# One stream of bodies through six layers: the feed-forward in pieces between the attention's tiles

## The reference, cut to what matters

```python
def layer(x):
    x = x + attn_layer(shift_tokens(x))
    return x + ffn_layer(shift_tokens(x))
# shift_tokens: channels 64 to 127 come from the token before
# attn_layer: q, k, v = x @ Wqkv; q and k to unit length, scaled, rotated;
#   each window of 32 tokens looks at itself and the window before it:
#   softmax(q @ k.T * 8 + mask) @ v; then @ Wo
# ffn_layer: xn = layernorm(x) * g + b; a, gate = split(xn @ W1 + b1)
#   (a * gelu(gate)) @ W2 + b2
```

## Time and profile before

| | us |
|---|---|
| median of three runs | 7222.45 |
| the profiled execution, its own time | 7208.77 |
| its span, first to last instruction | 7206.7 |
| mean granted TensorE clock over the span | 0.823 of 2.4 GHz |

### The profile page before, as it was taken

The page is one execution under the profiler, slowest core; times in us unless marked ns, Lnnn a source line. Parts: engine busy times, 40 slices in busy tenths (PEclk is TensorE's granted clock), DMA queues, the critical chain, the costliest instruction groups (busy, mean ns, idle before and its releaser), DMA issues. The chain is left out here.

```text
span 7206.7 us, 178920 instructions
## 1 busy us (share of the span) xinstructions
PE 5312.7 (74%) x69288; PEld 3368.6 (47%) x69288; DVE 3840.9 (53%) x6202; ACT 3985.0 (55%) x8451; POOL 2396.7 (33%) x1351
## 2 busy tenths in 40 slices
PE   1000198888888888977777988888888979687778
PEld 0000065655656564733333655656564747343444
DVE  5555654645455554555554645455554546445854
ACT  4333264646455555539997646555554546355655
POOL 0000162626354444504443626354453535000000
PEclk6555599999999999976666989999998989766876
DMA  1000121212222121200000212212121212000000
GB/s 43 0 0 0 37 51 48 55 49 54 53 49 59 42 53 50 57 11 1 1 1 20 55 47 53 54 45 52 47 57 44 57 45 57 18 2 3 0 2 6
DMA packets 177838, 248.52 MB, mean 34 GB/s; under 512 B 51692, under 2 KB 79848, under 8 KB 175080
## 3 DMA queue, kind: packets, MB, share of 16 engines
q1 hardware_dynamic: 177128, 237.68, 13.2%
HBM read 43.50 MB, written 5.24 MB: 7 GB/s over the span
## 5 line engine op out<-in xcount | busy, mean ns | idle before, releaser
L377 PE MATMUL PS<-arena 128*128 128x512 f32 x2304 | 1163.5, 632 | 220.0 <-ACT arena L500 117.1
L670 POOL TENSOR_TENSOR arena<-arena 128x512 f32<-128x512 f32 x384 | 586.6, 1551 | 651.3 <-DVE arena L622 651.3
L670 POOL TENSOR_TENSOR lns<-arena 128x512 f32<-128x512 f32 x384 | 566.1, 1498 | 666.7 <-DVE arena L622 666.7
L377 PEld LDWEIGHTS PS<-arena 128*128 128x128 f32 x2304 | 412.9, 199 | 646.1 <-issue 359.7
L499 ACT ACTIVATE arena<-PS 128x512 f32<-128x512 f32 x768 | 472.1, 615 | 333.4 <-PE PS L377 258.4
L434 PE MATMUL PS<-arena 64*64 64x32 f32 x24576 | 534.7, 227 | 155.4 <-ACT arena L531 121.4
L592 DVE TENSOR_REDUCE arena<-PS 128x16 f32<-128x1024 f32 x192 | 235.2, 1225 | 731.0 <-PE PS L408 731.0
L1106 PE MATMUL PS<-arena 128*128 128x512 f32 x8 | 6.7, 1019 | 807.8 <-DVE arena L1040 807.8
L434 PEld LDWEIGHTS PS<-arena 64*64 64x64 f32 x24576 | 509.5, 141 | 191.7 <-issue 188.0
L611 DVE TENSOR_REDUCE arena<-arena 128x32 f32<-128x2048 f32 x192 | 438.8, 2285 | 293.4 <-ACT arena L500 286.1
L539 ACT ACTIVATE arena<-PS 128x512 f32<-128x512 f32 x384 | 208.9, 597 | 648.0 <-PE PS L434 648.0
(11 more groups left out here) (254 smaller groups left out, 11101.2 us busy)
## 6 DMA issues: line engine op xcount, KB each, us to landing
arena<-arena SPq DMA_DIRECT2D x2880, 64.0 KB, 2.0
arena<-in_L_ffn_Wqkv SPq DMA_DIRECT2D x12, 1536.0 KB, 6.5
arena<-in_L_ffn_Wo SPq DMA_DIRECT2D x48, 128.0 KB, 6.3
scratch<-arena SPq DMA_DIRECT2D x4, 1024.0 KB, 4.8
arena<-scratch SPq DMA_DIRECT2D x4, 1024.0 KB, 7.6
arena<-in_L_ffn_W SPq DMA_DIRECT2D x12, 341.0 KB
arena<-in_ffn_scales SPq DMA_DIRECT2D x12, 128.0 KB, 5.8
arena<-in_L_ffn_W SPq DMA_DIRECT2D x12, 128.0 KB
```

The lines of the kernel that those rows point to most:

```text
L377: pe.matmul(PS[:, QKV + n % 2, :], xs[uu % 2][:, par * P:(par + 1) * P], w, start=True, stop=True).then_inc(qkv_ready, 1)
L670: last = pool.tensor_tensor(heads(t2)[:, :, a:a + 32], heads(raws[par])[:, :, b:b + 32], sine, ALU.mult)
```

## The change

All six layers of a call run as one stream, with no meeting between them. `body` is called for b = 0 to 3 of each layer, one after the other, with the work ahead reaching into the next layer. The feed-forward of the 512 tokens of body g - 1 (one chunk) runs in pieces inside body g. After the last body of the call the last chunk's feed-forward runs by itself.

- **TensorE.** The order in a tile is written out by hand for each of the four tiles. Projection chunks and turns alternate. `mean` and `variance` stand in tile 0, three `gate` pieces in tile 1, three `value` pieces in tile 2, two `down` pieces (256 tokens each) in tile 3; all use the two banks of the projection. Chunks 4 and 5 of a projection move behind the head products. The first half of `project` moves ahead of the second scores. The mask matmuls go.
- **ScalarE** writes the masks into the score banks (`write_mask`), makes the shifted copies, squares, takes the logarithm and exponential for one chunk in place in PSUM, copies the gates out with their bias, and takes gelu in two instructions from SBUF to SBUF, with a table load before and one behind. It copies v and takes the inverse norms at the end of a tile instead of before the probabilities. The three thirds of the next layer's `Wqkv` are loaded from its queue.
- **VectorE** centres, normalises (two instructions), gates and adds for one chunk a body. `unit_length` moves behind `softmax_shift` and `add_stream`.
- **GpSimd** does the sine product in one instruction over both halves, with the input's halves swapped. It makes the next layer's tables in the stream.
- **SP** puts the loads of scales, `Wo`, `W1` and `W2` between the windows' copies of the next bodies, each behind a wait for the last reader of the old weights.
- Outside the block some semaphores of `attn_a` are merged into others.

The diff, cut to its core. TensorE, tile 0 and the parts of the others that differ:

```diff
-            def body(g, final):
-                for tt in range(TILES):
...
+            def body(run, b, feed, final):
+                g = run * BODIES + b
+
+                chunk_read(g, 2, 4)
+                qkv(run, b, 3, 0, 0)
+                turn_qk(g, 1, 0)
+                chunk_read(g, 2, 5)
+                qkv(run, b, 3, 1, 1)
+                turn_qk(g, 1, 1)
+                chunk_read(g, 3, 0)
+                qkv(run, b, 3, 2, 0)
+                turn_qk(g, 1, 2)
+                if feed:
+                    chunk_read(g, 3, 1)
+                    mean(g, 1)
+                turn_qk(g, 1, 3)
+                chunk_read(g, 3, 2)
+                qkv(run, b, 3, 3, 0)
+                turn_probs(g, 0, final)
+                scores(g, 1, 0)
+                if feed:
+                    mean_read(g)
+                    variance(g, 1)
+                heads(g, 0, 0, final)
+                heads(g, 0, 1, final)
+                chunk_read(g, 3, 3)
+                qkv(run, b, 3, 4, 0)
+                scores(g, 1, 1)
...
+                qkv(run, b, 3, 5, 1)
...
+                turn_probs(g, 1, final)
+                scores(g, 2, 0)
...
+                    gate(run, b, 1, 1)
+                if feed:
+                    gate_read(g, 0)
+                    gate(run, b, 2, 0)
+                heads(g, 1, 0, final)
+                heads(g, 1, 1, final)
+                project(run, b, 0, 0)
...
+                    qkv(run, b, 4, 4, 1)
+                scores(g, 2, 1)
+                project(run, b, 0, 1)
...
+                heads(g, 2, 0, final)
+                heads(g, 2, 1, final)
+                if feed:
+                    value_read(g, 0)
+                    value(g, 2, 1)
...
+                    down(run, b, 1, 1)
+                heads(g, 3, 0, final)
+                heads(g, 3, 1, final)
+                project(run, b, 1, 0)
...
-            with pe.Fori(0, BODIES - 1) as it:
-                body(run * BODIES + it, False)
-            body(run * BODIES + BODIES - 1, True)
...
+            body(first, 0, False, False)
+            with pe.Fori(0, DEPTH - 1) as l:
+                for b in range(1, BODIES):
+                    body(first + l, b, True, False)
+                body(first + l + 1, 0, True, False)
```

The new functions of ScalarE, and its order in a tile:

```diff
+            def write_mask(g, tt):
+
+                S = PS[:, SCORE:SCORE + 2, :].rearrange("p s (m e) -> p (s m) e", e=FD)
+                act.activation(S, masks[:, tt % 2:tt % 2 + 1, :].broadcast_to([P, FH, 2 * WIN]), ACT.Copy)\
+                   .then_inc(mask_ready, 1)
...
+            def gelu(g):
+                act.wait_ge(gate_copied, nth(g - 1, M, M - 1))
+                act.activation(gl[:, 0:M - 1, :], gl[:, 0:M - 1, :], ACT.Gelu)
+                act.activation(gl[0:DIM[M - 1], M - 1, :], gl[0:DIM[M - 1], M - 1, :], ACT.Gelu).then_inc(gelu_ready, 1)
+                log_exp_tables(act)
...
                     if further:
-                        copy_qkv(g, tt + 3, (0, 1), True)
+                        copy_qkv(g, tt + 3, 0, PROJECTION_BANK[tt][0], True)
+                    if ahead:
+                        copy_turned(g, tt + 1, 0)
                     exps(g, tt)
+                    if further:
+                        copy_qkv(g, tt + 3, 1, PROJECTION_BANK[tt][1], True)
+                    if reload and tt == 0:
+                        load_projection(l, 0)
+                    if feed and tt == 0:
+                        shift(g, b)
                     if ahead:
-                        copy_turned(g, tt + 1, (0, 1))
+                        copy_turned(g, tt + 1, 1)
                     if further:
-                        copy_qkv(g, tt + 3, (2, 3), True)
+                        copy_qkv(g, tt + 3, 2, PROJECTION_BANK[tt][2], True)
                     if ahead:
-                        copy_turned(g, tt + 1, (2, 3))
+                        copy_turned(g, tt + 1, 2)
+                        write_mask(g, tt + 1)
+                        copy_turned(g, tt + 1, 3)
...
+                    if feed and tt == 0:
+                        square_centred(g)
+                    if feed and tt == 1:
+                        copy_gate(g, 0, 0)
                     copy_probs(g, tt, final)
+                    if feed and tt == 2:
+                        gelu(g)
```

VectorE, GpSimd and SP:

```diff
                 for tt in range(TILES):
+                    ahead = not (final and tt + 1 >= TILES)
+                    further = not (final and tt + 3 >= TILES)
                     softmax_norm(g, tt, nth(g, TURN_PER, place_probs(tt - 1, 1, False)))
-                    if not (final and tt + 3 >= TILES):
+                    if feed and tt == 0:
+                        centre(g, 1)
+                    if further:
                         norms(g, tt + 3)
-                        unit_length(g, tt + 3)
-                    if not (final and tt + 1 >= TILES):
...
+                    if ahead:
                         softmax_shift(g, tt + 1)
                     if tt % 2 == 1:
-                        add_stream(g, it, tt // 2)
...
+                        add_stream(g, b, tt // 2)
+                    if further:
+                        unit_length(g, tt + 3)
...
-                    for half in range(2):
-                        a, b = half * 32, 32 - half * 32
-                        sine = table[:, 2 + k, par:par + 1, a:a + 32].broadcast_to([P, FH, 32])
-                        last = pool.tensor_tensor(heads(t2)[:, :, a:a + 32], heads(raws[par])[:, :, b:b + 32], sine,
-                                                  ALU.mult)
-                    last.then_inc(t2_ready, 1)
+                    halves = lambda a: a.rearrange("p h (s e) -> p h s e", s=2)
+                    sine = halves(table[:, 2 + k, par:par + 1, :]).broadcast_to([P, FH, 2, 32])
+                    pool.tensor_tensor(halves(heads(t2)), halves(heads(raws[par]))[:, :, ::-1, :], sine, ALU.mult)\
+                        .then_inc(t2_ready, 1)
...
+                for tt in range(TILES):
+                    windows(g + 4, tt, False)
+                    if tt == 1:
+
+                        wait_alone(sp, o_ready, nth(g + 3, HEAD_PER, 9))
+                        load_output(ds(l + 1, 1))
```

More of the change, by code:

```diff
@@ L644, in fa_vector @@
[L644 to L656 removed]
+                norms(first * BODIES, tt)
@@ L872, in program @@
+            for b in range(2, BODIES):
+                for tt in range(TILES):
+                    windows((first + DEPTH - 1) * BODIES + b, tt, False)
         HD8 = 8
```

784 lines of the change are left out of this document (502 added, 282 removed).

## The result

The changed kernel takes 6547.9 us (median of 4 runs, 6545.28 to 6550.86) beside 7223.65 for the kernel before on the same chip: ratio 0.9065, 95% interval 0.9054 to 0.9076. The forecast was 6600. The profiled execution has a span of 6543.5 us, 663.2 less than before.

What follows compares the result with a forecast made beforehand. TensorE was taken to set the pace. Fills, 79.0 us bodies and ends made 1947.8 us a call, 654 us less over both; 7 back for the second call and 20 for borders gave 6600 us, range 6440 to 6850 (0.75).

Steps and rivals of the forecast that it cites:

- 8.7 against 7.7 us, just covered: First half of a tile: TensorE issues 8.7 us, ScalarE needs 7.7, so ScalarE is just covered except in tile 0.
- The body: One new steady body on TensorE, counted against an old one of 71.1 us: 79.05, taken as 79.0 us.
- Feed-forward pieces: One chunk's up-projection, down-projection, mean and variance on TensorE lengthen each body by 9.45 us.
- -2.4 of filled waits: Four TensorE waits of 0.6 us before the head products, now filled by feed-forward pieces: minus 2.4 us a body.
- Masks: Eight mask matmuls of 0.31 us leave TensorE, ScalarE writes the masks instead: minus 2.5 us a body.
- Output projection: Tiles 1 and 3: its first half waits for ScalarE's copy of the heads, 0.6 plus 0.2 us: plus 1.6 a body.
- Tile 0: ScalarE's two shift copies (0.96 us) stand ahead of the mean and stall TensorE: plus 0.6 us a body.
- VectorE and GpSimd: Normalised probabilities meet GpSimd's first sine product, delaying their turn about 0.3 us a tile: plus 1.2 a body.
- Gelu path and table loads: ScalarE's gelu and table switches in second halves: tightest in tile 2, 0.4 us a body, counted as nothing; 0.5 kept for range.
- Borders: Ten layer borders inside calls: new tables and weight loads cost 2 us each (bounds 0 and 8), 20 us in all.
- Ends of a call: Fill 45.65 us, first body without feed-forward 70.2, last body running dry 73.9, last chunk's feed-forward alone 20.
- TensorE never waits: Rival, chance 0.07: a body is TensorE's busy time alone, 74.6 us, giving 6390 us.

Runs made afterwards that it cites:

- up_twice: The changed kernel with each of the six up-projection pieces of a chunk issuing its matmul twice: 6754.78 us, ratio 0.9356.

## Why the prediction was right, and where its terms were off

By its steps:

- **What bounds it** held: TensorE sets the body, busy 76 of 78.1 to 79.6 us, and added work on it shows at eight to nine tenths (up_twice). It left out that ScalarE sets it as well: its 0.78 us more a tile showed at nine tenths too. My "8.7 against 7.7 us, just covered" compared the sums of a whole half. It took no account of the order within it: the second turned probabilities wait for a bank that ScalarE empties only behind the mask write, so of the 1.0 us 0.3 were left in tiles 1 and 2 and nothing in tile 0.
- **The body**, 79.0: measured 78.14 in the second call, 79.4 in most of the first. Feed-forward pieces: +9.45 of work, 8.3 in busy time; right as "what TensorE issues". The time it costs against no pieces at all is 3.5, since the -2.4 of filled waits was one of several such waits. I had added that waits return without pieces only for the head products, not for the turns. And it is luck that 79.0 came out so near. By my terms (71.1 - 2.5 + 1.6 + 1.2) a body of the stream without pieces has 71.4 us, and the pieces add 7.6 (9.45 - 2.4 + 0.6). Measured are 75.4 in the mean and 3.5: the first is 4 us too low, the second 4 too high, and they cancel. Of the first 4 us I estimate, from the waits and runs above, about 1 for the head products' gaps without a holder, 1.3 to 2.1 for the masks' term, and 0.5 for the jumps, which I had put at the borders; the rest is open.
- **Masks**, -2.5: mis-sized. Starts give 0.22 us each against the changed kernel, 1.76 a body, and 0.5 of it is lost again to ScalarE; the whole run shows 19 us, 0.4 a body, and the difference stays open. I took the distance from mask to scores, which holds 0.09 us that stay.
- **Output projection**, +1.6: measured 2 x 0.68 = 1.36; undone it gave 59 us.
- **Tile 0**, +0.6: measured 0.46 + 0.31 = 0.77, in the place named.
- **VectorE and GpSimd**, +1.2: the meeting is there, 1819 ns where 1227 had been the median, but TensorE's waits for it come to 0.4 us a body. That less came of it is read from waits; no run was without the meeting. The step named the delay and not what ends it; the argument that I used against the rival (ScalarE's copies hold the same step) applied to the term as well.
- **Gelu path and table loads**, 0: 0.3 us a body, as kept for the range. The swapped sine product takes 2.42 us where VectorE doesn't meet it, near the 2.5 taken.
- **Borders**, 2 us each: right in size, wrong in cause. Weight and table loads cost nothing that can be seen; the 20 us are eight jumps of ScalarE, which gave 3.3 us each when its loop was written out.
- **Ends of a call** (predicted in brackets): fill 44.3 (45.65), first body 69.4 (70.2), last body 67.5 and 70.1 (73.9), last chunk 26.8 and 27.3 (20). The last chunk's terms were read at clock 1.00, and it runs at 0.68: six up-projection instructions take 4.71 us there where twelve took 5.31:

```profile
2809.66 4.71 PE L491 MATMUL PS<-XN,arena 128*128 128x512 f32 x6 [2.99 <-issue]
```

The sum of a call was 1947.8 and the two are 1957.2 and 1941.9. The errors nearly cancel: the 22 bodies +11 in the first call and -7 in the second, last bodies -10, last chunks +14, fills and first bodies -4. The calls came to 3899.1 us for a predicted 3922.6 (3895.6, 20 for borders, 7 for a slower second call, which wasn't slower); 12 us lie outside of them, where I had nothing; and the median of the runs is 2.6 us over the profiled execution where it was 13.7. That is 47 of the 52 us between 6600 and 6547.9; the rest is my rounding. None of the three was foreseen, and that the two calls came so near is owed to errors that cancel.

Of the rivals, "TensorE never waits" (6390) is the one that the later kernels go towards: with the output projection late a body of the second call has 76.6 us, and with TensorE's loop written out as well one of either call 76.5. The one on the other side, banks handed over late by 0.4 us a piece, did not come; the projection's matmuls idle 25.8 us in all.

## What to carry to other kernels

Work that is moved into another stream costs what it adds on the bounding engine less the waits it fills; take it out of the new kernel and put it in twice, and both slopes are known (here 3.5 to 4.8 us for 8.3, then 4.7 for 5.15). Compare two engines by the order of their shared buffers, not by the sums of a half: a turn behind a bank that is emptied late leaves less room than the totals say. And when every n-th body is longer, count which one it is before a cause is named: here it was the loop's jump, not the border beside it.

## What was not expected of the hardware

- An engine's jump back over a long loop body costs it time with nothing in the profile to wait for: 2.1 to 2.7 us on ScalarE at the eight jumps of the changed kernel, and 0.7 to 1.4 us on TensorE, with another 1.3 to 1.9 just behind it in the second call. That it is the jump is shown by writing the loops out. On TensorE there were also gaps of 0.2 to 1.3 us inside the loop, in the head products, in the first call and nearly none in the second; written out, both are gone. Why the first call had them and the second not stays open.
- A VectorE operation with one input, 128x32 (L960), takes 738 ns in the mean in the changed kernel, up to 1.90 us, and 195 with GpSimd's sine product cut short (0.18 in the median): it is held by GpSimd's product too.
- From 128-row turns to the 64-row score matmuls TensorE spends 0.09 us, and a mask matmul put between them does not add to it (0.97 us without, 1.19 with it, and 0.31 from its start to the scores').
- GpSimd reads a half-swapped input at the cost of a straight one: 2.42 us (L1070) beside 2.37 (L1073), and 3.2 to 3.4 where VectorE's products meet either.
